# A cross-attention block: a pair's value products behind its own scores, three single score banks, four ring banks, and the last probability sums on VectorE

## What is computed

```python
x = x + xattn(layernorm(x), ctx_768, Wq, Wk, Wv, Wo, bo)
x = x + ffn(layernorm(x), router_w, router_b, sw1, sb1, sw2, sb2, rw1, rb1, rw2, rb2)
# xattn: q = x@Wq, k = ctx@Wk, v = ctx@Wv, per head of 64:
#        softmax(q k^T / 8) v, heads joined, @Wo + bo
# ffn:   gelu(x@sw1+sb1)@sw2+sb2 + sum over the top-2 experts of p_e*(gelu(x@rw1+rb1)@rw2+rb2)
```

## Time and profile before

| what | us |
|---|---|
| runs | 461.49, 462.86, 463.49; median 462.86 |
| profiled execution | 463.55, of which the span 461.7 |
| PE busy | 445.3 (96%) |
| POOL busy | 305.7 (66%) |
| DVE busy | 268.7 (58%) |
| ACT busy | 202.2 (44%) |

### The profile page before, as it was taken

One profiled execution on the slowest core, in us unless ns is written; L12 is line 12 of the kernel. 1 busy time (PEld: TensorE's weight loads), 2 busy tenths in 40 slices (PEclk: granted clock), 3 DMA queues, 4 the chain that ended last, 5 costly groups with the idle time before them and its releaser, 6 DMA issues. The chain is left out here.

```text
span 461.7 us, 7174 instructions
## 1 busy us (share of the span) xinstructions
PE 445.3 (96%) x2565; PEld 335.5 (73%) x2565; DVE 268.7 (58%) x550; ACT 202.2 (44%) x288; POOL 305.7 (66%) x204
## 2 busy tenths in 40 slices
PE   9998989999999999999999999999999889998996
PEld 7885767777776868786778676878776656776885
DVE  4697464956654848493546583937451319648443
ACT  3555131423453234153642332425514426687673
POOL 5969491949384486684864857666629678477672
PEclk9998989999999999999999999999999999999999
DMA  7300100000002000000030000000000000000000
GB/s 231 106 2 6 48 2 0 2 1 1 1 0 55 1 0 1 0 1 0 2 104 0 1 1 1 1 0 1 1 2 1 0 0 1 0 1 0 26 2 23
DMA packets 5194, 7.27 MB, mean 16 GB/s; under 512 B 644, under 2 KB 4136, under 8 KB 5160
## 3 DMA queue, kind: packets, MB, share of 16 engines
q1 hardware_dynamic: 5160, 6.81, 5.0%
HBM read 6.29 MB, written 0.52 MB: 15 GB/s over the span
## 5 line engine op out<-in xcount | busy, mean ns | idle before, releaser
L851 DVE TENSOR_REDUCE maxes<-ps 128x1 f32<-128x402 f32 x256 | 134.4, 569 | 99.2 <-PE ps L1050 98.4
L727 ACT ACTIVATE probs<-ps 128x1024 f32<-128x1024 f32 (+1 forms) x112 | 107.2, 962 | 178.0 <-PE ps L1122 175.8
L498 POOL TENSOR_TENSOR work<-work,probs 128x1024 f32<-128x1024 f32 x60 | 143.0, 2384 | 17.6 <-ACT probs L727 14.7
L496 POOL TENSOR_TENSOR work<-probs 128x1024 f32<-128x1024 f32 x15 | 35.9, 2393 | 93.7 <-issue 87.8
L1137 PE MATMUL ps<-probs,v_sb 128*64 128x256 f32 (+1 forms) x832 | 93.8, 382 | 0.0
L1120 PE MATMUL ps<-g_hi,ctxT_hi 97*128 97x512 f32 (+1 forms) x208 | 85.0, 409 | 3.7 <-DVE g_hi L859 2.0
L1137 PEld LDWEIGHTS ps<-probs,v_sb 128*64 128x64 f32 (+1 forms) x832 | 58.5, 137 | 33.8 <-issue 6.2
L1121 PE MATMUL ps<-g_lo,ctxT_hi 96*128 96x512 f32 (+1 forms) x208 | 82.8, 398 | 0.0
L1122 PE MATMUL ps<-g_hi,ctxT_lo 96*128 96x512 f32 (+1 forms) x208 | 82.6, 397 | 0.0
L1050 PE MATMUL ps<-ctxT_hi,g_hi 96*128 96x402 f32 x256 | 78.1, 370 | 0.8 <-DVE g_lo L847 0.4
L1050 PEld LDWEIGHTS ps<-ctxT_hi,g_hi 96*128 96x128 f32 x256 | 47.4, 191 | 19.9 <-DVE maxes L851 5.1
(11 more groups left out here) (147 smaller groups left out, 550.6 us busy)
## 6 DMA issues: line engine op xcount, KB each, us to landing
raw<-in_ctx_T_dram SPq DMA_DIRECT2D x3, 600.4 KB, 4.5
work<-in_L_ffn_rw_dram SPq DMA_DIRECT2D x1, 1024.0 KB, 7.9
raw<-in_ctx_T_dram SPq DMA_DIRECT2D x3, 150.8 KB, 2.9
x_sb<-in_x_dram SPq DMA_DIRECT2D x1, 384.0 KB, 5.9
early<-in_WqkT_dram SPq DMA_DIRECT2D x1, 336.0 KB, 5.3
wo_sb<-in_L_xattn_Wo_dram SPq DMA_DIRECT2D x1, 256.0 KB, 5.0
out_dram<-x_sb SPq DMA_DIRECT2D x1, 256.0 KB, 2.2
out_dram<-x_sb SPq DMA_DIRECT2D x2, 128.0 KB, 1.7
```

Of the source, the lines that this page charges most:

```text
L496: ops.tensor_tensor(acc, probs[:, (n - 1) % SLOTS], pr, ALU.add).then_inc(summed, 1)
L498: ops.tensor_tensor(acc, acc, pr, ALU.add).then_inc(summed, 1)
L727: nc.scalar.activation(probs[0:rows, n % SLOTS, 0:wide, :], s, ACT.Exp, scale=SCALE).then_inc(probs_ready, 1)
L851: v.tensor_reduce(maxes[:, p % 2, i * T + t, blk:blk + 1], src[:, 0:BW], AX.X, ALU.max).then_inc(ring_taken, 1)
```

## The change

- Values of a pair stand right behind its own 13 scores, with `sums` behind them; SLOTS is 7 in place of 8.
- Scores use three single banks (0 to 2) in turn, and each chunk has its own exponential (208 activations of 512 columns, in place of 96 of 1024 and 16 of 512).
- The ring has four banks (3 to 6) while scores run, three in the other stretches; the bank is the one used longest ago.
- VectorE takes the two closing additions of every pair, at the place where the values begin, the additions of units 4 and 5 of pair 13 and all of pairs 14 and 15. GpSimd keeps the first five of pairs 0 to 12.
- All `v` tasks of a batch stand in its first pair, one per chunk of scores. The shifts are placed by the planner when the maxima are out, at the latest ahead of their own scores.
- `w2` casts move from the last pair to the one before, `wrow` of the second half one turn earlier, ahead of the `second` products of that turn.

```diff
-RING = 3
+RING = 4
+SCORE_BANKS = 3
-SLOTS = 8
+SLOTS = 7
...
         for u, unit in enumerate(units):
             for j, c in enumerate(unit):
-                if vs and (u or p):
-                    main.append(("ring", ("v",) + vs.pop(0)))
+                if p == 0 and b:
+                    main.append(("ring", ("v", b, c)))
                 main.append(("scores", (b, p, u, j)))
-                if n and (u, j) in ((1, 0), (2, 0)):
-                    main.append(("quotient", order[n - 1] + (u - 1,)))
+                if n and u < 2 and j == 1:
+                    main.append(("quotient", order[n - 1] + (u,)))
...
-            if n and u == 0:
-                main += held + [("sums", order[n - 1])]
-                held = []
...
-            if (b, p) == order[-1]:
+            if (b, p) == order[-2]:
                 main += [("w2", e) for e in range(experts) if e * n_units // experts == u]
...
+        main += held + [("sums", (b, p))] * (n + 1 < len(order))
+        held = []
...
+                if shifts and last_max[shifts[0]] <= done:
+                    task = ("shift",) + shifts[0]
+                    must = kind == "scores" and w[:2] == shifts[0] or last_max[shifts[0]] + 8 <= done
+                    if must or max(max_end[shifts[0]], free[-RING]) <= pe and not (v_at[0] - i < 8 and apart):
+                        put(("ring", task))
...
+            pe = max(pe, shift_end.get((w[0], w[1]), 0.0), exp_end.get(n_exp - SCORE_BANKS, 0.0)) + PE_US["scores"]
...
-            if h == 1 and turn == 0:
-                out.append(("ring", ("wrow", last)))
...
+    for n, (kind, w) in enumerate(steps):
+        if kind == "ring":
+            k = len(ring_banks)
+            wide = n in amid
+            bank = min(range(O_BANK - (RING if wide else 3), O_BANK), key=lambda i: held.get(i, -1))
+            ring_banks.append(bank)
+            ring_last.append(held.get(bank))
+            held[bank] = k
...
-        def s_bank(n, c):
-            return ps[:, 2 * (n % 2) + c, :]
+        def s_bank(n):
+            return ps[:, n % SCORE_BANKS, :]
...
+        def adds(pair, u):
+
+            return "dve" if u == NU - 1 or pair >= B * PAIRS - 2 or pair == B * PAIRS - 3 and u >= 4 else "pool"
...
+                if kind == "scores" and w[3] == 1 and adds(w[0] * PAIRS + w[1], w[2]) == "dve":
                     add_probabilities(v, dve, then_own, w)
+                if kind == "values" and w[2:] == (0, 0):
+
+                    add_probabilities(v, dve, then_own, (w[0], w[1], NU - 1, 0))
...
-                        if n >= 2:
-                            pe.wait_ge(probs_ready, n - 1)
+                    if n >= SCORE_BANKS:
+                        pe.wait_ge(probs_ready, n - SCORE_BANKS + 1)
```

More of the change, by code:

```diff
@@ L63, in plan @@
                   for k in range(blocks)]
-        put = dict(late)
+        put = {}
         if n == 1:
@@ L160, in put @@
             shift_end[w[1:3]] = dve + HOP_US
-    last = None
-    for x in main:
+    last, apart = None, 0
+    v_at = [i for i, x in enumerate(main) if x[0] == "ring" and x[1][0] == "v"] + [len(main) + 9]
+    for i, x in enumerate(main):
         kind, w = x
+        if v_at[0] <= i:
+            v_at.pop(0)
+            apart = 0
         if kind == "scores" or kind == "values" and last != "values":
-            need = last_of[("shift", w[0], w[1])] if kind == "scores" else 0
+            need = last_max[w[:2]] if kind == "scores" else 0
             n = index[w[0], w[1]] + (w[2] + 1) / n_units + LEAD
-            while done < len(tasks):
+            while done < len(tasks) or shifts:
+                if shifts and last_max[shifts[0]] <= done:
[3 more added lines that the diff above has]
+                        put(("ring", task))
+                        apart += 1
+                        shifts.pop(0)
+                        continue
+                if done == len(tasks):
+                    break
                 task = tasks[done]
                 pair = task[1] * pairs + task[2] if len(task) > 2 else 0
-                at = max(free[-RING], ready(task)) if event(task)[0] == "ring" else pe
+                at = free[-RING] if event(task)[0] == "ring" else pe
                 if done >= need and (at > pe or pair > n or task[0] == "max" and task[1] not in split):
                     break
+                if done >= need and v_at[0] - i < 8 and apart and event(task)[0] == "ring":
+                    break
+                apart += event(task)[0] == "ring"
                 put(event(task))
@@ L176, in plan @@
         if kind == "scores":
[L177 to L184, removed]
+            pe = max(pe, shift_end.get((w[0], w[1]), 0.0), exp_end.get(n_exp - SCORE_BANKS, 0.0)) + PE_US["scores"]
+            act = max(act, pe + HOP_US) + EXP_US
+            exp_end[n_exp] = act + HOP_US
+            n_exp += 1
             out.append(x)
         elif kind == "values":
-            pe += PE_US["values"] + (TILING_US if last != "values" else 0.0)
+            if last != "values":
+                pe += TILING_US
+                dve = max(dve, pe + ADDED_US) + DVE_US["add"]
+            pe += PE_US["values"]
             out.append(x)
@@ L281, in build @@
     nth = {w: k for some in sorts for k, w in enumerate(some)}
+    O_BANK = 7
+    kinds = [kind for kind, _ in steps]
+    amid = range(kinds.index("scores"), len(kinds) - kinds[::-1].index("values"))
+    ring_banks, ring_last, held = [], [], {}
+    for n, (kind, w) in enumerate(steps):
[6 more added lines that the diff above has]
+            held[bank] = k
+    LAST_OF_3 = max(k for k, bank in enumerate(ring_banks) if bank == 3)
     def quarter(i):
```

73 lines of the change are left out of this document (33 added, 40 removed).

## The result

The changed kernel takes 456.38 us (median; 455.28 to 458.91), the kernel before 463.18 us in the same comparison: ratio 0.984, 95% interval [0.980, 0.988]. I had said 452.8 in a range of 447.5 to 459. Direction and range held. The gain is 6.8 us where I worked out 10, and a large part of it comes from other causes than I said.

What follows compares the result with a forecast made beforehand. TensorE, busy 445.3 of 461.7 us, was taken to bound the kernel. Gains of 14.4 less losses of 3.8 net 10.6, kept as 10: span 451.7, median forecast 452.8 us, range 447.5 to 459.

Steps and rivals of the forecast that it cites:

- Point 1: End of pair 0: row sums wait for GpSimd's late fifth addition and VectorE's closing two; loss 3.0 us (0.8 to 5).
- Points 2, 5 and 6: End of pair 1, other shifts, and seams behind lone chunk 12: TensorE's waits go; gains 3.5, 1.3 and 2.0 us.
- point 2: End of pair 1: shift behind the batch removes idle time, waits and half clock; gain 3.5 us.
- Point 3: v tasks in first pairs: short exponentials and a fourth bank end waits for ScalarE's copies; gain 2.9 us.
- Point 4: Row sums of pairs 13 and 14: VectorE adds there, so TensorE's idle time goes; gain 3.1 us.
- Point 7: The wrow copy: TensorE's wait goes, but it may stand 0.4 for the router's ranking; gain 0.6 us (0 to 1).
- Point 8, the fourth bank: Fourth ring bank: saves a third of the extra time between scores in 12 pairs; gain 1.0 us (0 to 3).
- Point 9: Row sums of pairs 1 to 12: due sooner, so short new waits in some pairs; cost 0.4 us (0 to 5).
- Rival A: Row sums wait for the closing additions in every pair, no scores standing between; 466 us, chance 0.07.
- Point 10: Single score banks and w2 casts: scores wait for exponentials only in pair 14; cost 0.4 us (0 to 1).
- rival C: Single score banks make TensorE wait at each chunk, which leaves no gain; 462.5 us, chance 0.06.
- Rival B: VectorE, not the number of banks, held the ring, so its gains shrink; 458 us, chance 0.15.

Runs made afterwards that it cites:

- e7: Changed kernel with only pair 0's values, row sums and quotients in the old place, and eight slots of probabilities; 451.02 us, ratio 0.973.
- e3: Changed kernel with 32 small matmuls, their output overwritten, between batch and row sums of pair 0; 454.36 us, ratio 0.977.
- e10: Changed kernel with the four context pieces of the next batch moved from the first to the second pair of each batch; 462.06 us, ratio 0.997.
- e8: e2 with the shifts behind the third maximum of the next pair, as before the change; 449.86 us, ratio 0.970.
- e2: Changed kernel with values, row sums, quotients and v tasks in their old places, and eight slots; 449.83 us, ratio 0.967.
- e5: e2 with three ring banks in place of four; 466.89 us, ratio 1.001.
- e9: e6 with three ring banks in place of four; 470.00 us, ratio 1.013.
- e6: e2 with all additions of pairs 0 to 14 back on GpSimd, VectorE adding only in the last pair; 460.65 us, ratio 0.993.
- e12: e2 with the two closing additions of pairs 0 to 12 on GpSimd; 451.05 us, ratio 0.974.
- e1: Changed kernel with the two closing additions of pairs 0 to 12 back on GpSimd; 465.19 us, ratio 1.003.

## Why the prediction was right, and where not

- **Point 1, the end of pair 0** was seen with its mechanism and its times: fifth addition to 46.9 (47.2), 0.69 each on VectorE (0.65), sums at 48.44 (48.7). Against the kernel before its size was right too, 3.0. The last chunk of pair 1 starts 3.4 us later in the changed kernel, with one max more done (0.2), so 3.2 lost. TensorE there, in the kernel before:

```profile
62.18 0.40 PE L1120 MATMUL ps<-g_hi,ctxT_hi 97*65 97x512 f32 x1
```

In the changed kernel:

```profile
65.59 0.40 PE L1149 MATMUL ps<-g_hi,ctxT_hi 97*65 97x512 f32 x1
```

In e7, which leaves pair 0 in its old place (three maxima more done than before, 0.5):

```profile
60.68 0.40 PE L1155 MATMUL ps<-g_hi,ctxT_hi 97*65 97x512 f32 x1
```

So the old place gains 2.0 us with the new banks, because the stalls that I left inside the 51.03 (the half clock and most waits) go without any move. That is what I missed: the price of the place is 5.4 (e7), not 3. Inside the term the clock was off: I took one short stretch (1.7) behind a stand four times as long. It was twice as long, up to 3.4, of which e3 gave back 2.0 to 2.5. The reason I gave for GpSimd's lateness is wrong: it is through with the weights at 24.7, waits twice for VectorE's moments, and starts at 30.92; e10 shows that it is the 16 us of work from there on (five additions, four context pieces, a pow) that count.
- **Points 2, 5 and 6 (6.8 us)** named the right waits, which are gone, but the wrong cause. (The terms of point 2 add up to 3.4, not 3.5.) I said that the shift moved behind the batch and the batch into the seam; e8 has neither, and is as fast as e2. What removes the waits are the new banks. With three ring banks the shifts still wait 2.7 us at two places (e5 and e9), with four they don't (e2). No score waits for an exponential in any of these four, so the single score banks do that part. The scores' row falls by 7.1 us in the changed kernel and by 6.9 in e2. The clock loss of point 2 came back in point 1.
- **Point 3** held. The loader's 4.8 us went to 0.2. The `v` matmuls themselves fell by 1.1 us. The waits ahead of them stand in the scores' row: from the last matmul of a chunk to the `v` task behind it TensorE spends 11.5 us before, at 36 places, and 8.3 after. That makes 4.3 us, where I had 2.9. Both figures, 8.3 and 37.0, are the same in e2, e5, e6 and e9. So neither the place in the first pair, nor the fourth bank, nor VectorE's additions are the cause; what all of these have is the short exponentials, which point 3 named. No run takes those away alone.
- **Point 4** held: 1.83 and 1.68 from the last value to the row sums became the ordinary 0.2, 3.1 us. What I had not priced is that the moved `w2` splits make this part necessary: without VectorE's additions pairs 13 and 14 cost 9.6 us (e6 against e12). No run leaves the splits where they were.
- **Point 7** held, 0.32 idle in place of 0.9.
- **Point 8, the fourth bank (1.0, bounds 0 to 3)**, is the worst-sized term. I read its worth from an undisturbed pair with three banks, VectorE not adding, and a third of 0.3 to 0.6 us in 12 pairs is 1.2 to 2.4, not 1.0. With this order e9 says 9.3 and e5 12 to 17. It is more than the net gain of the change, because with three banks the clock is lost in long stretches (12.6 us of clock loss in either run), which a pair without a stand can't show.
- **Point 9 (0.4)**: the sums' waits outside pair 0 come to 2.4 us on the loader, at four places; the longest is in pair 10, 1.25 us (0.79 on TensorE). The margin of point 9 was nearly right. Rival A's chain (additions, row sums, no scores between) is real: e1, which makes it about 1 us longer, stands at 465.2, where I had 466.
- **Point 10**: no score waits for an exponential; rival C falls. Rival B's worry that VectorE holds the ring fits e5, where banks are few; with four banks the maxima cost 2.4 us more in place of a gain.

In sum the right total came partly from errors against each other: the place, which I had bring some 2 us net, costs 6.5; the fourth bank, which I had at 1, is worth 9 or more. The runs can be read as a chain from the kernel before to the changed one: 463.2; single score banks with three ring banks, the planner's shifts, the moved `w2` splits and `wrow` (e9) 470.0; fourth ring bank (e6) 460.7; VectorE's additions (e2) 449.8; the new place 456.4. Its first step is not taken apart. It has the gains of points 3 and 6, and against them a stand of 5.1 us in pair 14 and long stretches at 1.2 GHz; no run has the single score banks alone. Why a given series of waits brings the clock down and another does not stays open: e8 passes 1.22 us idle with a mean clock of 1.000, e5 loses it behind 1.72 and 1.56, and the kernel before does either in different executions.

## What to carry to other kernels

Read a change of several parts as a table of corners, not as a sum: here one part (closing additions on VectorE) is worth 9 us or 1 by where another stands, and the fourth bank 9 or 12 to 17. When a consumer is moved ahead of work that used to hide its producer, list the first pair by itself, with everything that stands in the producer's queue from its start; an exception for one pair gave back 5.4 of 6.5 us. Ask of each stall that a part is to remove whether another part removes it anyway. When times are summed from start to start, look for a wait in the row of the instruction ahead of it. Price a stand with the clock behind it, and look at the mean granted clock of each variant before explaining its time by idle stretches.

## Unexpected of the hardware

A small VectorE operation can stand for a whole GpSimd addition. VectorE's timeline in the changed kernel, a product over 32 columns:

```profile
276.43 2.12 DVE L932 TENSOR_TENSOR rprob<-lexp,rsum 128x32 f32<-128x32 f32 x1
```

GpSimd's at the same time:

```profile
276.12 2.39 POOL L527 TENSOR_TENSOR work<-work,probs 128x1024 f32<-128x1024 f32 x1 [0.72 <-ACT probs L754]
```

They end together, and the product takes 2.12 us where one of the kernel before took 0.39. In e5 it is a scalar operation on two columns with one tensor input, which takes 0.16 elsewhere. VectorE's timeline:

```profile
345.99 2.38 DVE L823 TENSOR_SCALAR veps<-mv 128x2 f32<-128x2 f32 x1
```

GpSimd's, whose second addition ends with it:

```profile
343.47 4.87 POOL L529 TENSOR_TENSOR work<-work,probs 128x1024 f32<-128x1024 f32 x2 [1.95 <-ACT probs L756]
```

TensorE then stood 0.87 us behind it, then 0.48 and 0.92 behind VectorE's own additions of 1.21 each, and ran at 1.2 GHz from 351 to 361. The Trainium skill, page "SBUF — State Buffer", section "Who interferes with whom", says that GpSimd and VectorE lock each other out both for VectorE instructions with two SBUF inputs and for scalar operations that enter a two-port mode. Both rows agree with it, though no view names the mode of the second. My prediction had weighed the rule for the additions alone, not for the short operations on the path to a maximum.
